# Two edge stages of a graph network: products paired in PSUM banks, scores three items behind, softmax chain one item later

## The reference

```python
# stages 0 and 1 (4 heads of 64)
xl, xr = x @ Wl, x @ Wr
e = leaky_relu(xl[src] + xr[dst], 0.2)
logits = einsum('ehc,hc->eh', e, att)
ex = exp(logits - segment_max(logits, dst)[dst])
out = segment_sum(xl[src] * ex / segment_sum(ex)[dst], dst) + b
# stage 2 (8 heads of 32)
e = leaky_relu(s1[src] + s2[dst], 0.2)          # then the same softmax and sum
```

## Time and profile before

| what | value |
|---|---|
| median of 3 runs | 4043.88 us (4042.95 to 4047.39) |
| span of the profiled execution | 5270.5 us (no other time of that execution is listed) |
| PE busy, matmul | 3942.9 us, 75% of the span |
| DVE busy | 3296.7 us, 63% |
| POOL busy | 2645.7 us, 50% |
| ACT busy | 1199.0 us, 23% |
| mean granted clock of TensorE | 0.887 |

### The profile page before, as it was taken

How to read it: one execution, slowest core, us unless ns; L and a number is a source line. 1 busy time by engine, 2 the same in 40 slices (tenths; PEclk the granted TensorE clock), 3 DMA queues, 4 the chain that set the end, 5 groups by cost and what they waited for, 6 DMA issues and landing times. The chain is left out here.

```text
span 5270.5 us, 122213 instructions
## 1 busy us (share of the span) xinstructions
PE 3942.9 (75%) x31349; PEld 2833.8 (54%) x31350; DVE 3296.7 (63%) x9997; ACT 1199.0 (23%) x4200; POOL 2645.7 (50%) x2941
## 2 busy tenths in 40 slices
PE   6588878888878795888887888787566666666666
PEld 5355555565655574555555556555344444444443
DVE  6466666666666762666666666666466666666666
ACT  3322222222222362222222222223100000000002
POOL 4455555555555224555555555543455555555550
PEclk8799999999899997999999999989777777777779
DMA  3333333333333123333333333325444434343333
GB/s 91 97 95 98 96 98 95 97 93 93 96 96 99 50 66 88 98 94 99 95 98 92 100 94 98 94 77 156 118 110 109 110 106 112 108 111 108 108 106 104
DMA packets 333905, 521.10 MB, mean 99 GB/s; under 512 B 152887, under 2 KB 219617, under 8 KB 333809
## 3 DMA queue, kind: packets, MB, share of 16 engines
q0 software_dynamic: 120320, 338.39, 23.8%
q1 hardware_dynamic: 213489, 181.58, 12.1%
HBM read 484.14 MB, written 35.46 MB: 99 GB/s over the span
## 5 line engine op out<-in xcount | busy, mean ns | idle before, releaser
L692 POOL DMA_INDIRECT gathered<-table,idx x2496 | 2452.7, 983 | 2090.4 <-POOLq L358 1516.7
L1130 PE MATMUL pS<-gathered,Dm 128*128 128x264 f32 x4992 | 1860.0, 456 | 193.2 <-issue 63.0
L1527 DVE TENSOR_TENSOR acc_mem<-acc_mem,pS 128x264 f32 x2496 | 1048.2, 420 | 466.8 <-remote 224.2
L1069 PE MATMUL pZ<-DT,x 128*128 128x128 bf16 x9984 | 1206.0, 229 | 167.1 <-ACT reluT L864 99.3
L1069 PEld LDWEIGHTS pZ<-DT,x 128*128 x9984 | 926.6, 102 | 598.2 <-issue 341.3
L864 ACT ACTIVATE reluT<-pZ 128x256 f32<-128x256 f32 x1664 | 610.2, 382 | 1990.8 <-PE pZ L1075 1248.1
L1130 PEld LDWEIGHTS pS<-gathered,Dm 128*128 128x128 f32 x4992 | 876.0, 218 | 324.5 <-issue 146.8
L1075 PE MATMUL pZ<-ident,gathered 128*128 128x128 f32 x3328 | 972.5, 292 | 18.0 <-issue 10.7
L1558 DVE TENSOR_TENSOR gathered<-gathered 128x256 f32<-128x256 f32 x2496 | 945.8, 419 | 60.6 <-ACT gathered L856 28.8
L1083 PE MATMUL pL<-reluT,attpad 128*32 128x128 f32 x6656 | 277.5, 286 | 408.4 <-ACT reluT L864 373.3
L1540 DVE TENSOR_TENSOR Dm<-pS,rel_items 128x256 f32<-128x256 f32 x1239 | 515.0, 416 | 0.0
(11 more groups left out here) (232 smaller groups left out, 3335.0 us busy)
## 6 DMA issues: line engine op xcount, KB each, us to landing
DT<-rel_dram SPq DMA_DIRECT2D x156, 512.0 KB
gathered<-table,idx POOLq DMA_INDIRECT x2496
flags<-flag_dram SPq DMA_DIRECT2D x1664, 8.0 KB
span_row<-flag_dram SPq DMA_DIRECT2D x1664, 0.1 KB
table<-xls SPq DMA_DIRECT2D x147, 132.0 KB
flags<-flag_dram SPq DMA_DIRECT2D x416, 32.0 KB
gathered<-table SPq DMA_DIRECT2D x98, 132.0 KB, 2.1
gathered<-in_x SPq DMA_DIRECT2D x98, 128.0 KB, 2.1
```

The lines of the kernel that those rows point to most:

```text
L692: nc.gpsimd.indirect_dma_start(out=G[:, b, i, :], out_offset=None, in_=tab[l], in_offset=bass.IndirectOffsetOnAxis(ap=idx[:, b, i:i + 1], ...
L1069: mm = nc.tensor.matmul(z_slot(i)[:, half], x3[:, bass.ds(tk[i], 1), s, half].rearrange("p o c -> p (o c)"), moving, start=(s == 0), stop= ...
L1130: nc.tensor.matmul(pS[:, i % 4, 0:ROW], Dm[:, i % 8, :], G[:, at[0], at[1], :], start=True, stop=True).then_inc(seg_done, 1)
L1527: link(v.tensor_tensor(acc_at(n), acc_at(n), pS[:, n % 4, 0:ROW], ALU.add))
```

## The change

In stages 0 and 1 two items share a bank of `pZ`: items 2j and 2j + 1 write its two halves, only the second posts `zt_done`, and ScalarE reads both with one ReLU of 512 columns (`relu_pair`). `expand` of an even item waits for the pair four items back. `scores(k)` stand at i = 6, 10, 14, and `scores(3)` at i = 1 of the next group. The steps of the chain on TensorE and ScalarE stand one item later (`after(l)`, `LOGITS = 1`): logits at 1, ends at 3, carries at 5, `dif` at 7, the rescaling at 9 and 10. VectorE's parts stay at the ends of the same steps. In all three stages the drop of the maximum, which waits for `m_ready`, moves ahead of the multiplications of step 3, and `me` is copied directly behind the exponentials. `rel_items` is kept in bf16, and `reluT` grows from five to six slots.

```diff
-        rel_items = sb("rel_items", [P, ITEMS])
+        rel_items = sb("rel_items", [P, ITEMS], BF16)
...
-        reluT = sb("reluT", [P, 5, D])
+        reluT = sb("reluT", [P, 3 * 2, D])
...
+        def relu_pair(i):
+
+            pair = 1 if i % Q > 1 else i // Q % 2 * 2
+            return reluT[:, 2 * pair:2 * pair + 2, :].rearrange("p i c -> p (i c)")
+
         def relu_slot(i):
-
-            return reluT[:, 4 if i % (2 * Q) == Q else i % Q, :]
+            return relu_pair(i)[:, i % 2 * D:(i % 2 + 1) * D]
...
+        def z_pair(i):
+
+            return pZ[:, i // 2 % 2, 0:2 * D]
+
         def z_slot(i):
-
-            return pZ[:, i % 2, 0:D]
+            return z_pair(i)[:, i % 2 * D:(i % 2 + 1) * D]
+
+        def after(l):
+
+            return LOGITS if l < 2 else 0
...
-                        if first and l < 2:
+                        if first and l < 2 and i % 2:
                             act.wait_ge(zt_done, up(zt_done))
-                            nc.scalar.activation(relu_slot(i), z_slot(i), ACT.Relu).then_inc(relu_done, 1)
-                        if second and i == 2:
+                            nc.scalar.activation(relu_pair(i), z_pair(i), ACT.Relu).then_inc(relu_done, 1)
+                        if second and i == 2 + after(l):
                             act.wait_ge(ends_turned, up(ends_turned))
...
-                        if l < 2 and i % Q != 1 and (second or i >= 2):
+                        if l < 2 and i % 2 == 0 and (i >= Q or second and i < LOGITS + 1):
                             pe.wait_ge(relu_done, up(relu_done))
...
-                        mm.then_inc(zt_done, 1)
+                        if i % 2:
+                            mm.then_inc(zt_done, 1)
...
-                        if second and i == 6:
+                        if second and i == 6 + after(l):
                             pe.wait_ge(dif_ready, up(dif_ready))
...
-                        if second and i == 0:
+                        if second and i == after(l):
                             if l < 2:
                                 scores(K4 - 1, 1 if first else 2)
                             pe.wait_ge(lin_ready, up(lin_ready))
...
-                        if first and l < 2 and i > 0 and i % Q == 0:
-                            if second and i == Q:
+                        if first and l < 2 and i > Q and i % Q == 2:
+                            if second and i == Q + 2:
                                 pe.wait_ge(logits_copied, up(logits_copied))
-                            scores(i // Q - 1, 1)
+                            scores(i // Q - 1, 0)
...
-                            if i == 2:
+                            if i == 2 + after(l):
                                 pe.wait_ge(scan_done, up(scan_done))
...
-                            if i == 4:
+                            if i == 4 + after(l):
                                 pe.wait_ge(carry_ready, up(carry_ready))
...
-                            if i == 8:
+                            if i == 8 + after(l):
                                 pe.wait_ge(fx_ready, up(fx_ready))
...
+                        if second and s == 3:
+
+                            dve.wait_ge(m_ready, up(m_ready))
...
+                            v.tensor_scalar(fr[0:1, 1, 0:H], fr[0:1, 0, 0:H], 0.0, None, ALU.min).then_inc(drop_ready, 1)
                         if at:
                             if p == GI // 4:
                                 dve.wait_ge(ex_ready, up(ex_ready))
```

More of the change, by code:

```diff
@@ L846, in body @@
                             linear(c)
-                        if second and i == 0:
+                        if second and i == 2 * after(l):
                             act.wait_ge(logits_done, up(logits_done))
@@ L857, in body @@
                                                      ACT.Exp).then_inc(ex_ready, 1)
-                        if second and i == 9:
+                            nc.scalar.activation(me[:], pM[:, 0:P], ACT.Copy).then_inc(m_ready, 1)
+                        if second and i == 9 + after(l):
                             act.wait_ge(fx_spread, up(fx_spread))
@@ L875, in body @@
                             nc.scalar.activation(first_row[:, 1:2], DT[:, c, 0:1], ACT.Copy, scale=-1.0, bias=1.0).then_inc(dt_free, 1)
-                        if second and i == 6:
-                            nc.scalar.activation(me[:], pM[:, 0:P], ACT.Copy).then_inc(m_ready, 1)
-                        if second and i == 7:
+                        if second and i == 7 + after(l):
                             act.wait_ge(drop_ready, up(drop_ready))
@@ L1099, in body @@
                                              start=False, stop=True).then_inc(logits_done, 1)
-                        if first and l < 2 and i > 0 and i % Q == 0:
-                            if second and i == Q:
+                        if first and l < 2 and i > Q and i % Q == 2:
+                            if second and i == Q + 2:
                                 pe.wait_ge(logits_copied, up(logits_copied))
-                            scores(i // Q - 1, 1)
-                        if second and not first and i == 1:
+                            scores(i // Q - 1, 0)
+                        if second and not first and i == after(l) + 1:
                             pe.wait_ge(logits_copied, up(logits_copied))
@@ L1551, in body @@
                                 v.memset(end_row[:], -BIG).then_inc(edge_done, 1)
+                        if second and s == 3:
+                            dve.wait_ge(m_ready, up(m_ready))
+                            top = me[0:1, :].rearrange("o (h i) -> o h i", h=8)[:, :, 0] if l == 2 else heads_first(me[0:1, :])[:, :, 0, 0]
+                            link(v.tensor_tensor(fr[0:1, 0, 0:H], by_head(end_row[:, 0])[:, :, 0], top, ALU.subtract))
+                            if l < 2:
+                                last = last_items[:, bass.ds(k0 - GI, GI)].rearrange("p (k a) -> p k a", a=Q)
+                                v.tensor_tensor(G[:, c, :, D + 4:ROW].rearrange("p (k a) h -> p k a h", a=Q),
+                                                me[:].rearrange("p (a h k) -> p k a h", a=Q, h=8)[:, :, :, 0:4],
+                                                last.unsqueeze(3).to_broadcast([P, K4, Q, 4]), ALU.mult)
+                            linked()
+                            v.tensor_scalar(fr[0:1, 1, 0:H], fr[0:1, 0, 0:H], 0.0, None, ALU.min).then_inc(drop_ready, 1)
                         if at:
@@ L1654 @@
 IOTA = 288
+LOGITS = 1
 def kernel(**inputs):
```

13 lines of the change are left out of this document (2 added, 11 removed).

## The result

The changed kernel takes 4493.12 us (4490.1 to 4496.9), the kernel before 4045.64 us beside it: a ratio of 1.111 [1.109, 1.112], 447 us slower. The forecast was 4444 us, range 4200 to 4590, slower.

A forecast was written before the change was run, and what follows sets the result against it. TensorE, with 19.9 us of work per group and hardly any stall, was taken as the bound. Stalls of 4.46 us less 0.5, about 3.9 x 102 groups = 400 us, gave 4044 + 400 = 4444 us, range 4200 to 4590.

The forecast's parts named there:

- The four stalls: TensorE, first two stages: per group S(2) waits 1.07 us, S(4) 1.67, S(6) 0.4, S(7) 1.32; sum 4.46.
- The 0.5: Taken off the 4.46 us per group for what a group loses today (0 to 1 us) and can lose inside the stalls.
- C: TensorE, carries to S(6): distance 2.4 us against 1.97 of covering work after the change, stall 0.4 us per group.
- It does; zero: Stage 2: `me` before the multiplications costs VectorE 0.2 to 0.4 us per group, covered by POOL's 20.0; priced zero.
- POOL's 20 us: POOL's gathers, 0.95 + 0.30 = 1.25 us each back to back, take 20.0 us per group.
- The profile's own: First profile: the other 9 us of a 29.3 us group were mostly from profiling, with late semaphores, absent in timed executions.
- The forecast span of 5250 to 5700: Changed kernel's profile: waits for late ReLUs (3.5 us per group) fall away while 4.46 come in; span 5250 to 5700 us.
- the waits on the ReLUs were real: Rival, TensorE ahead of the scores: a fifth of those waits, 0.7 us per group, is real; gains 71 us, 3973; chance 0.10.
- The group: TensorE's work in one group of the edge stages, added up from unwaited starts: 19.9 us.
- the prediction's own last sign: If POOL's gathers run back to back at 1.25 us through a stage, POOL paces it and the rest is hidden.
- no difference: Rival: POOL's gathers pace the stages at 20 us and TensorE has room, so the time stays; chance 0.04.
- Posts: Eight fewer semaphore posts per group: no price seen; by the skill's 26 ns each, 0.2 us per group, about 20 us back.

The follow-up runs named there:

- chain_late_only: Kernel before with nothing but the chain one item later in the first two edge stages: 4396.3 us, ratio 1.088.
- before_again: Kernel before, unchanged, profiled a second time on the chip where it takes 5234 us: 5229.67 us, profile span 5227.8.
- before_look: Kernel before, unchanged, profiled on a chip where it takes 4044 us: 4042.16 us, span 4040.3.
- pairs_only: Against the kernel before: only the pairs, the scores' later place, bf16 item numbers and earlier `me`; no late chain, no drop ahead: 4054.12 us, ratio 1.003.
- drop_ahead_only: Changed kernel with the chain back at its old items (LOGITS = 0), drop of the maximum still ahead of the multiplications: 4107.08 us, ratio 1.015.

## Why the prediction was right, and where it was off

**The mechanism held.** In the changed kernel TensorE's own list bounds the first two stages, as forecast. The four stalls stand at the four places named, in every group, and in the group shown each is within 0.2 us of its forecast. The decisive experiment is *chain_late_only*: the late chain alone costs 353 us, and in the other direction, without it the changed kernel is at 4107.

**The sum.** Forecast 4.46 us of stalls, less 0.5 (3.96, taken as 3.9), so 400 us for the two stages. Measured 3.93 in the group shown, and 3.8 on average, 390 us. The 0.5 was taken off for stalls that groups lose today. TensorE's idle time of today is 0.3 us (1085 less 1069.48, over 51); the other part of the agreement comes from distances that were all too long, by 0.07 to 0.28 us. One cost was not in the sum: an S that has waited takes longer itself, S(2) 0.55 us (1021.65 to 1022.20) against 0.45 for S(1) (1019.70 to 1020.14). That the total came within 10 us in these stages is in part luck. C was half as large as forecast: the carries cost 0.14 us there (1001.55 to 1001.69), not the 0.38 of their record, and its distance was 2.12, not 2.4.

**The drop ahead of the multiplications in stage 2: "It does; zero".** This is the step that failed, and it makes most of the 49 us between forecast and result: it cost 54. The step priced what VectorE loses and held POOL's 20 us against it as cover. But POOL was the stage's limit, so nothing covered POOL, and the price came through the gathers themselves: more of them started over a multiplication, and took longer there. With 1.25 us per gather from one undisturbed row I took the shortest pitch for the mean: before, the group is 20.8 us, not 20.0.

**"The profile's own".** Wrong. That the first profile was 30% longer than the timed runs, I put down to profiling. *before_again* has 5229.67 us timed and 5227.8 in the profile, with the same "remote" waits, and *before_look* has 4042.16 and 4040.3, without any. So it is the chip, or the machine around it, on which the kernel ran; the slow one was met only once, so chip and moment can't be told apart. The forecast span of 5250 to 5700 for the changed kernel falls with it. The forecast survived because it took only durations and distances from undisturbed stretches and made its sum against 4044. The rival "the waits on the ReLUs were real" is true on the chip with 5234 us, where the pairs give 2.8%, and false on the others.

**The group.** 19.9 us was added up from the fastest pieces (the terms give 19.8); it is 21.3. POOL's 20.0 was too short as well: its gathers take 1.33 us each in these stages, 21.3 us per group, and run back to back. By the prediction's own last sign, gathers back to back, POOL paced the kernel before; it does not pace the changed one. The rival "no difference" was right that POOL paces these stages today; it fell because the room for the stalls was a few tenths of a us, not 4. On TensorE some expands simply take longer; in *before_look* the one that starts at 1001.17:

```profile
1001.17 0.47 PE L1069 MATMUL pZ<-DT,x 128*128 128x128 bf16 x3
...
1001.99 0.28 PE L1075 MATMUL pZ<-ident,gathered 128*128 128x128 f32 x1
```

The scores follow at 1002.19, so it took 1.02 us where the neighbours take 0.56, at a clock of 1.00; what slows it stays open. Both errors did little harm to a difference of two kernels, but they harm the argument about room ("TensorE 19.9, POOL 20.0"): neither engine had any.

**Priced at zero and found so:** the ReLU of 512 columns took 597 ns (0.60 forecast) and cost nothing that shows, and bf16 for `rel_items` left `Dm` at 413 ns (414 in *before_look*). Posts showed no price: *pairs_only*, which has fewer, is 10 us slower than before, not 20 faster, and in it an expand with the post and one without both take 0.56 to 0.57 us from start to start.

## What to carry to other kernels

Where a bound engine sends something off and later needs the answer, write down the distance of the round trip and the work that covers it, before moving either end; here each trip took 2.0 to 2.9 us, and one item moved, with what stood there, took 0.7 to 2.0 us of cover away and opened a stall in all four, since the cover had been longer than the trip only by some tenths. Add such stalls up only on the engine that has no room, and look for a second price on the engine that paces the other stages, even if the edit is on a third one; take that engine's mean over a whole stage and not its shortest row. When a profile is much longer than the timed runs, profile the kernel again, on another chip, before explaining either.

## What the runs showed of the hardware

- One program takes 4044 us on some chips and 5234 on another. There, ScalarE has waits named "remote" (149.7 us in 900, up to 4.7 us at once), and TensorE is busy 652.58 of 800 us (500 to 1300, granted clock 0.95), against 790.20 in the same stretch of *before_look* (clock 1.00). The cause is open. An edit can be worth 2.8% on the one and nothing on the other, or cost 8.8% on the one and 0.8% on the other.
- An indirect gather of 128 rows occupies POOL for 0.95 us and 0.30 between two; behind the moved drop two in each 16 take 1.45 and 1.80. Only gathers that start over certain VectorE operations are longer: started over a multiplication of two SBUF operands 1.24 us on average in *drop_ahead_only*, already running when one starts 0.945. The multiplications are not longer for it (0.412 us).
- TensorE's two small products of the carries are listed with 0.28 us in the changed kernel and cost 0.14 from start to next start (0.24 on average in *before_look*); only starts add up.
- An S takes 0.55 us to the next start after a wait (1021.65 to 1022.20 in the changed kernel) and behind the scores (1010.61 to 1011.16), and 0.45 behind an expand without one (1012.74 to 1013.18).
